# Sharing PSUM banks in the rotation and the layernorm, and a tail that waits for the last addition, in a transformer layer on eight cores

## The chip, the cores and the metric

The kernel runs on 8 cores of one Trainium2 chip, in one launch. Every core works on one sequence of 2048 tokens and holds all weights' slices in turn; the cores exchange nothing. The metric is the device time in microseconds of the slowest core. In this text PE is TensorE, DVE is VectorE, ACT is ScalarE, POOL is GpSimd, and SP is the engine from whose queue the loads of x and the stores of the output are issued.

## The reference

One layer: attention with rotary embedding on a layernormed x, then a mixture of experts (8 routed, top 2, and one shared) on a layernormed sum.

```python
def _rope(x):                      # even, odd: the two halves of the head's 128
    return concatenate([even * cos - odd * sin, even * sin + odd * cos])

q = _rope(einsum('btm,mhd->bthd', x, w_aq))
k = _rope(einsum('btm,mhd->bthd', x, w_ak))
v = einsum('btm,mhd->bthd', x, w_av)
s = einsum('bihd,bjhd->bhij', q, k) / 128 - 1e30 * causal_mask
r = einsum('bhij,bjhd->bihd', softmax(s), v) @ w_ao
...
shared_out = (silu(xf @ sw1) * (xf @ sw3)) @ sw2
cw = top-2 softmax weights of xf @ router_w.T
moe_out = einsum('te,teh,ehd->td', cw, silu(g) * u, w2)
...
x = x + attn(layernorm(x))         # 2048 x 1024 per core, 8 heads of 128
x = x + ffn(layernorm(x))          # 8 experts, 1 shared, hidden 2048
```

## The kernel before

All instructions of an engine stand in one list, in the order in which the Python code emits them, and every engine works through its list in that order. `bank_prod` emits a PE instruction that fills a PSUM bank: it waits for the tokens given to it and for everything in `bank.frees`, the instructions that read the bank since it was last filled. `bank_cons` emits a reader: it waits for the bank's last fill and adds itself to `frees`. There are eight banks, `ps[0]` to `ps[7]`, of 128 x 512 f32.

The activations are kept transposed (channels on partitions) in `x_sb` (f32) and `xn_sb` (bf16), in eight chunks of 128 channels (`kc`) by 2048 tokens, and the tokens are taken in four groups of 512 (`ts`).

The stages in order:

- x is loaded and transposed by PE through `ps[0]` and `ps[1]` (line 311), DVE copies it to `x_sb`.
- `layernorm` (lines 337 to 422), for each `ts`: DVE casts eight chunks (L355), PE sums them over the channels in `bank_s` (L364), DVE squares them (L376), PE sums the squares in `bank_q` (L380), DVE and ACT work out mean and inverse deviation on one row, PE spreads the two rows over the partitions in `bank_a` and `bank_b` (L402, L405), DVE copies these out (L408, L410), POOL scales and shifts (L415, L418). The banks alternate with the parity of `ts`. It is called twice, ahead of the attention and ahead of the experts.
- `emit_qkv_rope(h)` for each of the 8 heads, once for q and once for k, so 16 blocks. In a block PE projects all four token groups into `ps[0]` to `ps[3]` (32 matmuls, L486). Then, for each `ts`: DVE copies the bank to bf16 (L497), PE multiplies that copy by the rotation matrix into a bank of its own, `ps[4]` or `ps[5]` (L501), DVE multiplies the projection by the cosines (L506) and the rotated copy by the sines (L510), and POOL adds the two products (L514). The two products have one buffer each, so L506 of the next group waits for the POOL addition of this one (`t_rot_prev`).
- The order of the attention on PE: values of four heads, block q and block k of head 0, and then for each head `emit_passA(h)` (a bound for the softmax), `emit_qkv_rope(h + 1)`, `emit_passB(h)` (scores into `ps[4]` and `ps[5]` (L601), causal mask added by DVE (L607), exponentials by ACT (L613), product with the values (L587) and row sums (L592)). The weights of head h + 2 are requested on POOL's queue between the last two.
- Output projection, second layernorm, router.
- The experts, nine times: 16 chunks of gate and up projections (L877, L890), then eight chunks of the down projection (L938), each followed by four additions of DVE into `x_sb` (L947).
- The tail: PE transposes `x_sb` back through `ps[0]` and `ps[1]`, 128 transposes (L974), DVE copies each to a staging buffer (L980), four stores of 2 MB leave on SP's queue. The order is four groups of 512 tokens, and in each `kc` outside and the four token tiles inside; a transpose waits for the last addition of its own chunk, `t_xfinal_dc[kc]`.

Of the kernel before, what the change touches and what calls it, by code (L numbers as in the profile page):

```python
# [19 lines left out]
KC = DM // 128  # L20
# [97 lines left out]
def build_nc(dbg=False):  # L118
# [32 lines left out]
    x_sb = nc.alloc_sbuf_tensor("x_sb", [128, KC * T], F32)  # L151
# [35 lines left out]
    bigf = big[:, :].bitcast(F32)  # L187
# [3 lines left out]
    ps = [PsBank(nc.alloc_psum_tensor(f"ps{i}", [128, 512], F32).ap()) for i in range(8)]  # L191
# [32 lines left out]
    def bank_prod(bank, fn, waits=(), last=True):  # L224
        w = list(waits) + bank.frees
        toks = b.emit("tensor", fn, waits=w, incs=[(pe, 1)] if last else ())
        bank.frees = []
        if last:
            bank.ready = toks[0]
            return toks[0]  # L230
        return None
# [105 lines left out]
    def layernorm(t_x_tok, per_ts=None):  # L337
        if not isinstance(t_x_tok, list):
            t_x_tok = [t_x_tok]
        xn_tok = []  # L340
        U0 = sf[0:1, 2048:2560]
        U1 = sf[0:1, 2560:3072]
        U2 = sf[0:1, 1536:2048]
        a_rep = sf[:, 0:512]
        b_rep = sf[:, 512:1024]
        tmp = sf[:, 1024:1536]
        t_gp_prev = None
        for ts in range(NTS):
            tcol = ts * 512
            t_cp = None  # L350
            for kc in range(KC):
                col = kc * T + tcol
                t_cp = b.emit("vector",
                              lambda e, o=xn_sb[:, col:col + 512],
                              i=x_sb[:, col:col + 512]: e.tensor_copy(o, i),  # L355
                              waits=(per_ts[ts] if per_ts else t_x_tok),
                              incs=[(dv, 1)])[0]
            bank_s = ps[(ts % 2) * 2]
            for kc in range(KC):
                col = kc * T + tcol  # L360
                bank_prod(bank_s,
                          lambda e, r=xn_sb[:, col:col + 512],
                          s0=(kc == 0), s1=(kc == KC - 1):
                          e.matmul(bank_s.ap[0:1, :], onesb[:, :], r, start=s0, stop=s1),  # L364
                          waits=[t_cp], last=(kc == KC - 1))
            t_sum = bank_s.ready
            xsq = [sf[:, 2560 + i * 256: 2560 + (i + 1) * 256].bitcast(BF16)
                   for i in range(2)]
            bank_q = ps[(ts % 2) * 2 + 1]
            t_xsq_pe = [None, None]  # L370
            for kc in range(KC):
                xa = xsq[kc % 2]
                col = kc * T + tcol
                w = [t_cp, t_xsq_pe[kc % 2]]
                t_sq = b.emit("vector",
                              lambda e, o=xa, i=xn_sb[:, col:col + 512]: e.tensor_mul(o, i, i),  # L376
                              waits=w, incs=[(dv, 1)])[0]
                tokp = bank_prod(bank_q,
                                 lambda e, r=xa, s0=(kc == 0), s1=(kc == KC - 1):
                                 e.matmul(bank_q.ap[0:1, :], onesb[:, :], r, start=s0, stop=s1),  # L380
                                 waits=[t_sq], last=True)
                t_xsq_pe[kc % 2] = tokp
            t_ssq = bank_q.ready
            t1 = b.emit("vector", lambda e: e.tensor_scalar_mul(U0, bank_s.ap[0:1, :], 1.0 / DM),
                        waits=[t_sum], incs=[(dv, 1)])[0]
            bank_s.frees.append(t1)
            t2 = b.emit("vector", lambda e: e.tensor_scalar_mul(U1, bank_q.ap[0:1, :], 1.0 / DM),
                        waits=[t_ssq], incs=[(dv, 1)])[0]
            bank_q.frees.append(t2)
            b.emit("vector", lambda e: e.tensor_mul(U2, U0, U0), incs=[(dv, 1)])  # L390
            b.emit("vector", lambda e: e.tensor_sub(U1, U1, U2), incs=[(dv, 1)])
            t3 = b.emit("vector", lambda e: e.tensor_scalar_add(U1, U1, EPS),
                        incs=[(dv, 1)])[0]
            t4 = b.emit("scalar", lambda e: e.activation(U2, U1, AF.Ln),
                        waits=[t3], incs=[(ac, 1)])[0]
            t5 = b.emit("scalar", lambda e: e.activation(U1, U2, AF.Exp, scale=-0.5),
                        waits=[t4], incs=[(ac, 1)])[0]
            t6 = b.emit("vector", lambda e: e.tensor_scalar_mul(U2, U0, -1.0),
                        waits=[t5], incs=[(dv, 1)])[0]
            t7 = b.emit("vector", lambda e: e.tensor_mul(U0, U2, U1), incs=[(dv, 1)])[0]  # L400
            bank_a, bank_b = ps[4 + (ts % 2)], ps[6 + (ts % 2)]
            bank_prod(bank_a, lambda e: e.matmul(bank_a.ap[:, :], ones1[:, :], U1,  # L402
                                                 start=True, stop=True),
                      waits=[t5, t6, t_ones1])
            bank_prod(bank_b, lambda e: e.matmul(bank_b.ap[:, :], ones1[:, :], U0,  # L405
                                                 start=True, stop=True),
                      waits=[t7])
            ta = bank_cons(bank_a, "vector", lambda e: e.tensor_copy(a_rep, bank_a.ap[:, :]),  # L408
                           waits=[t_gp_prev])
            tb = bank_cons(bank_b, "vector", lambda e: e.tensor_copy(b_rep, bank_b.ap[:, :]))  # L410
            t_last = None
            for kc in range(KC):
                col = kc * T + tcol
                tm = b.emit("gpsimd",
                            lambda e, i=x_sb[:, col:col + 512]: e.tensor_mul(tmp, i, a_rep),  # L415
                            waits=[ta, t_sum, t_ssq, t_last], incs=[(gp, 1)])[0]
                t_last = b.emit("gpsimd",
                                lambda e, o=xn_sb[:, col:col + 512]: e.tensor_add(o, tmp, b_rep),  # L418
                                waits=[tb, tm], incs=[(gp, 1)])[0]
            t_gp_prev = t_last  # L420
            xn_tok.append(t_last)
        return xn_tok
# [20 lines left out]
    rope_t1 = [sf[:, 1024 + i * 512: 1024 + (i + 1) * 512] for i in range(2)]  # L443
    scale_rep = sf[:, 2048:2560]
    invl_row = sf[0:1, 2560:3072]
    invl_row_bf = sbf[0:1, 5120:5632]
    mh_row = mh_sb[0:1, 0:8]
    qb_free_tok = [None] * 2
    t_rot_prev = [None]
# [21 lines left out]
    def emit_qkv_rope(h):  # L471
        par = h % 2
        for which in range(2):
# [15 lines left out]
            for ts in range(NTS):  # L489
                sl = ts % 2  # L490
                bank = ps[ts]
                pqb = ps[4 + sl]
                qb = rope_qb[sl]
                tcs = csn[:, ts * 512:(ts + 1) * 512]
                tsn = csn[:, T + ts * 512: T + ts * 512 + 512]
                te = bank_cons(bank, "vector",
                               lambda e, o=qb, i=bank.ap[:, :]: e.tensor_copy(o, i),  # L497
                               waits=[qb_free_tok[sl]])
                qb_free_tok[sl] = bank_prod(pqb,
                                            lambda e, o=pqb.ap[:, :], r=qb:  # L500
                                            e.matmul(o, pmat_sb[:, :], r,  # L501
                                                     start=True, stop=True),
                                            waits=[te, t_pmat])
                t_t1a = bank_cons(bank, "vector",
                          lambda e, o=rope_t1[0], i=bank.ap[:, :], c=tcs:
                          e.tensor_mul(o, i, c),  # L506
                          waits=[t_cs, t_rot_prev[0]])
                t_t1b = bank_cons(pqb, "vector",
                          lambda e, o=rope_t1[1], i=pqb.ap[:, :], c=tsn:
                          e.tensor_mul(o, i, c),  # L510
# [316 lines left out]
        w2_tok[(widx, dc)] = dma(wd_w2[par], "gpsimd", dst, src, waits=[w2_free[par]])  # L827

    eo_mul_tok = [None, None]
    t_xfinal_dc = [None] * KC  # L830
    pf_w1(0, 0)
    pf_w3(0, 0)
    pf_w1(0, 1)
# [5 lines left out]
    for ei, e_ in enumerate(e_order):  # L839
# [85 lines left out]
        for dc in range(KC):  # L925
            par = dc % 2
            bset = ps[4 * (dc % 2): 4 * (dc % 2) + 4]
            for hc in range(16):
                for tsx in range(NTS):
# [8 lines left out]
                              e.matmul(o, l, r, start=s0, stop=s1),  # L938
                              waits=[w2_tok[(widx, dc)], t_eo],
                              last=(hc == 15))  # L940
            tadd = None
            for tsx in range(NTS):
                bank = bset[tsx]
                xcol = dc * T + tsx * 512
                tadd = bank_cons(bank, "vector",
                                 lambda e, o=x_sb[:, xcol:xcol + 512], i=bank.ap[:, :]:
                                 e.tensor_add(o, o, i))  # L947
            if ei == len(e_order) - 1:
                t_xfinal_dc[dc] = tadd
            w2_free[par] = (pe, pe.n)  # L950
            nxt = dc + 2
            if nxt < KC:
# [3 lines left out]
    t_final = (dv, dv.n)  # L956

    out_tiles = d["out"].rearrange("(g p) m -> p g m", p=128)
    stage = [bigf[:, 8192:12288], bigf[:, 12288:16384]]
    stage_free = [None, None]  # L960
    slot = 0
    for g4 in range(4):
        par = g4 % 2
        evac_toks = []
        for kc in range(KC):
            for ti in range(4):
                tt = g4 * 4 + ti
                bank = ps[slot % 2]
                sl = (slot // 2) % 4
                pap = bank.ap[:, sl * 128:(sl + 1) * 128]  # L970
# [1 line left out]
                bank_prod(bank,  # L972
                          lambda e, o=pap, i=x_sb[:, col:col + 128]:
                          e.transpose(o, i, identf[:, :]),  # L974
                          waits=[t_xfinal_dc[kc], stage_free[par]])
                evac_toks.append(
                    bank_cons(bank, "vector",
                              lambda e,
# [58 lines left out]
```

How the kernel before makes its waits and increments, by code:

```python
        def run(e, ws=ws, fn=fn, rincs=rincs):  # L75
            for sem, v in ws:
                e.wait_ge(sem, v)
            inst = fn(e)
            for sem, amt in rincs:
                inst = inst.then_inc(sem, amt)
```

## Time and profile before

| | |
|---|---|
| median of 12 runs | 4812.16 us (4803.93 to 5417.91) |
| the profiled execution's own time | 4818.27 us |
| its span, core 1, the slowest | 4816.7 us |
| the other cores' spans | 4797.3 to 4815.8 us |
| PE busy | 4036.8 us (84%), 16618 matmuls |
| DVE busy | 1557.1 us (32%) |
| ACT, POOL busy | 581.5 us (12%), 668.8 us (14%) |
| chain that ended last | PE 79%, DVE 12%, issue 3%, POOL 3%, ACT 2%, DMA 1% |
| mean granted TensorE clock, core 1 | 0.883 of full |

The span is the time from the first to the last instruction of a core. A busy share is taken over the whole span; the chain of work that ended last is followed back from the last instruction, at each step to what released it, and says which engine's time is on the path.

### The profile page before, as it was taken

Reading aid. Unit: us, or ns where it says so; the run is one execution under the profiler, and the core shown is the slowest. Engines: PE = TensorE matmul, PEld = TensorE weight load, DVE = VectorE, ACT = ScalarE, POOL = GpSimd, SP = SyncE. Lnnn points to the kernel's source line nnn. Section 1 sums busy time; section 2 is a strip of 40 time slices with the busy share of each in tenths; the row PEclk is TensorE's granted clock in tenths of the full one; section 3 lists DMA queues with packets and bytes.
Section 4 is the critical chain, followed back from the end, with each engine's and each line's share of the span. In section 5 each row is a group of like instructions: output and inputs, shape, how many; then the busy total and the mean of one; then the engine's idle time right before and its main releaser. Section 6 shows DMA issues by size and latency. Waiting matters only on the chain.

```text
span 4816.7 us, 48360 instructions; the slowest of 8 cores (4797.3 to 4816.7 us)
## 1 busy us (share of the span) xinstructions
PE 4036.8 (84%) x16618; PEld 1666.1 (35%) x16618; DVE 1557.1 (32%) x2517; ACT 581.5 (12%) x933; POOL 668.8 (14%) x649
## 2 busy tenths in 40 slices
PE   5266566566574699999999999999999999999998
PEld 2021112111121244444444444444444444444443
DVE  4633333333336332232332332322322322322323
ACT  0002220112220110010110110110110100100100
POOL 0621101111104310010110110110110110111100
PEclk9576677677686799999999999999999999999986
DMA  4000000000010343343343443433433434343422
GB/s 99 0 9 5 5 5 5 5 0 5 3 13 3 31 38 38 36 40 35 36 40 36 37 38 37 39 36 35 40 35 36 40 36 38 37 39 37 40 27 75
DMA packets 480622, 142.95 MB, mean 30 GB/s; under 512 B 473722, under 2 KB 476026, under 8 KB 480386
## 3 DMA queue, kind: packets, MB, share of 16 engines
q0 software_dynamic: 475488, 122.72, 27.7%
q1 hardware_dynamic: 4898, 17.14, 1.0%
q8 instruction: 141, 2.31, 0.2%
q14 instruction: 95, 0.78, 0.1%
HBM read 254.12 MB, written 8.39 MB: 54 GB/s over the span
## 4 chain that ended last, share of the span: by engine, by line
PE 79%; DVE 12%; issue 3%; POOL 3%; ACT 2%; DMA 1%; DVEq 0%; POOLq 0%; ACTq 0%; SPq 0%
PE ps L938 21%; PE ps L877 21%; PE ps L890 21%; PE ps L486 3%; DVE s_sb L622 2%; PE ps L587 2%; PE ps L592 2%; PE ps L601 2%; PE ps L626 1%; DVE xn_sb L355 1%; POOL pT L534 1%; PE ps L462 1%; ACT pT L613 1%; PE ps L671 1%; POOL big L514 1%
## 5 line engine op out<-in xcount | busy, mean ns | idle before, releaser
L877 PE MATMUL ps<-xn_sb,w_sb 128*128 128x512 bf16 x4608 | 1062.7, 384 | 5.9 <-DVE s_sb L861 3.5
L938 PE MATMUL ps<-big,w_sb 128*128 128x512 bf16 x4608 | 1029.6, 388 | 25.5 <-DVE big L912 25.5
L890 PE MATMUL ps<-xn_sb,w_sb 128*128 128x512 bf16 x4608 | 1041.5, 379 | 0.0
L907 DVE TENSOR_TENSOR s_sb<-ps,s_sb 128x512 bf16<-128x512 f32 x512 | 354.1, 692 | 1181.5 <-PE ps L890 1154.9
L221 POOL DMA_DIRECT2D w_sb<-w x360 | 333.9, 931 | 2769.6 <-PE ps L890 1778.3
L938 PEld LDWEIGHTS ps<-big,w_sb 128*128 128x128 bf16 x4608 | 458.8, 100 | 596.2 <-issue 108.0
L898 ACT ACTIVATE s_sb<-ps 128x512 bf16<-128x512 f32 x576 | 344.0, 597 | 2618.1 <-PE ps L877 2586.6
L877 PEld LDWEIGHTS ps<-xn_sb,w_sb 128*128 128x128 bf16 x4608 | 454.8, 99 | 567.7 <-issue 37.3
L890 PEld LDWEIGHTS ps<-xn_sb,w_sb 128*128 128x128 bf16 x4608 | 450.8, 98 | 543.7
L947 DVE TENSOR_TENSOR x_sb<-x_sb,ps 128x512 f32<-128x512 f32 x288 | 197.9, 687 | 857.5 <-PE ps L938 833.8
L613 ACT ACTIVATE pT<-ps,negmh 128x512 bf16<-128x512 f32 x320 | 220.0, 688 | 681.1 <-DVE ps L607 412.7
L912 DVE TENSOR_TENSOR big<-s_sb 128x512 bf16<-128x512 bf16 x576 | 245.0, 425 | 63.0 <-DVE s_sb L907 3.7
L587 PE MATMUL ps<-pT,big 128*128 128x512 bf16 x320 | 145.7, 455 | 75.8 <-ACT pT L613 64.3
L607 DVE TENSOR_TENSOR ps<-ps,maskm 128x512 f32<-128x512 f32 x128 | 89.6, 700 | 276.9 <-PE ps L601 273.9
L601 PE MATMUL ps<-big 128*128 128x512 bf16 x320 | 154.6, 484 | 20.9 <-DVE s_sb L629 11.7
L626 PE MATMUL ps<-s_sb,ones 1*128 1x512 f32 x64 | 65.3, 1121 | 117.7 <-DVE s_sb L622 117.7
L534 POOL TENSOR_TENSOR pT<-big 128x512 bf16<-128x512 bf16 x64 | 66.4, 1038 | 595.6 <-PE ps L626 545.7
L486 PE MATMUL ps<-xn_sb,w_sb 128*128 128x512 bf16 x512 | 142.3, 446 | 1.6 <-DVE big L466 1.6
L592 PE MATMUL ps<-pT,onesb 128*1 128x512 bf16 x320 | 141.0, 441 | 0.0
L501 PE MATMUL ps<-s_sb,pmat_sb 128*128 128x512 bf16 x64 | 31.8, 497 | 121.6 <-DVE s_sb L497 121.6
L622 DVE RECIPROCAL s_sb<-ps 1x512 f32<-1x512 f32 x32 | 107.1, 3346 | 62.0 <-PE ps L592 62.0
L514 POOL TENSOR_TENSOR big<-s_sb 128x512 bf16<-128x512 f32 x64 | 80.7, 1261 | 293.1 <-DVE s_sb L510 293.1
(109 smaller groups left out, 1460.4 us busy)
## 6 DMA issues: line engine op xcount, KB each, us to landing
w_sb<-w POOLq DMA_DIRECT2D x288, 256.0 KB, 6.0
w_sb<-w POOLq DMA_DIRECT2D x72, 512.0 KB, 8.0
big<-x SPq DMA_DIRECT2D x4, 2048.0 KB, 13.9
out<-big SPq DMA_DIRECT2D x4, 2048.0 KB, 7.2
w_sb<-wv POOLq DMA_DIRECT2D x2, 1024.0 KB, 19.9
w_sb<-wq POOLq DMA_DIRECT2D x8, 256.0 KB, 6.0
w_sb<-wk POOLq DMA_DIRECT2D x8, 256.0 KB, 6.6
w_sb<-wo POOLq DMA_DIRECT2D x8, 256.0 KB, 4.8
```

What stands on the lines that cost most here:

```text
L221: return b.emit(eng, lambda e, o=out_ap, i=in_ap: e.dma_start(out=o, in_=i), waits=waits, incs=[(ch, 16)], nochain=True)[0]
L486: e.matmul(o, l, r, start=s0, stop=s1),
L587: e.matmul(o, l, r, start=s0, stop=s1_),
L592: e.matmul(o, onesb[:, :], r, start=s0, stop=s1_),
L601: e.matmul(o, l, r, start=True, stop=True),
L613: e.activation(o, i, AF.Exp, bias=negmh[:, 0:1], scale=1.0 / DH),
L877: e.matmul(o, l, r, start=s0, stop=s1),
L890: e.matmul(o, l, r, start=s0, stop=s1),
L898: lambda e, o=sb_b, i=gb_.ap[:, :]: e.activation(o, i, AF.Silu),
L907: e.tensor_mul(o, i, c),
L912: e.tensor_mul(o, a, bb),
L938: e.matmul(o, l, r, start=s0, stop=s1),
```

## The change

Four edits:

1. `layernorm` uses `ps[0]` to `ps[3]` for its four banks in every token group, where it alternated between two sets.
2. In `emit_qkv_rope` the rotated copy goes back into the bank that holds the projection. For that L506 (cosines) is emitted ahead of the rotation matmul L501, and L501 waits for it.
3. The tail's transposes wait for `t_final`, the last of all additions, where each waited for the last addition of its chunk; the two loops inside a group of 512 tokens change places.
4. The tail's staging buffers are the ones of the load at the start (`bigf[:, 0:8192]`) where they were `bigf[:, 8192:16384]`. An alias that nothing uses, `invl_row_bf`, is gone.

```diff
-            bank_s = ps[(ts % 2) * 2]
+            bank_s = ps[0]
...
-            bank_q = ps[(ts % 2) * 2 + 1]
+            bank_q = ps[1]
...
-            bank_a, bank_b = ps[4 + (ts % 2)], ps[6 + (ts % 2)]
+            bank_a, bank_b = ps[2], ps[3]
...
-    invl_row_bf = sbf[0:1, 5120:5632]
...
             for ts in range(NTS):
                 sl = ts % 2
                 bank = ps[ts]
-                pqb = ps[4 + sl]
+                pqb = bank
                 qb = rope_qb[sl]
...
                 te = bank_cons(bank, "vector",
                                lambda e, o=qb, i=bank.ap[:, :]: e.tensor_copy(o, i),
                                waits=[qb_free_tok[sl]])
+                t_t1a = bank_cons(bank, "vector",
+                          lambda e, o=rope_t1[0], i=bank.ap[:, :], c=tcs:
+                          e.tensor_mul(o, i, c),
+                          waits=[t_cs, t_rot_prev[0]])
                 qb_free_tok[sl] = bank_prod(pqb,
                                             lambda e, o=pqb.ap[:, :], r=qb:
                                             e.matmul(o, pmat_sb[:, :], r,
                                                      start=True, stop=True),
-                                            waits=[te, t_pmat])
-                t_t1a = bank_cons(bank, "vector",
-                          lambda e, o=rope_t1[0], i=bank.ap[:, :], c=tcs:
-                          e.tensor_mul(o, i, c),
-                          waits=[t_cs, t_rot_prev[0]])
+                                            waits=[te, t_t1a, t_pmat])
                 t_t1b = bank_cons(pqb, "vector",
                           lambda e, o=rope_t1[1], i=pqb.ap[:, :], c=tsn:
                           e.tensor_mul(o, i, c),
...
-    t_xfinal_dc = [None] * KC
...
-            if ei == len(e_order) - 1:
-                t_xfinal_dc[dc] = tadd
...
-    stage = [bigf[:, 8192:12288], bigf[:, 12288:16384]]
-    stage_free = [None, None]
     slot = 0
     for g4 in range(4):
         par = g4 % 2
         evac_toks = []
-        for kc in range(KC):
-            for ti in range(4):
-                tt = g4 * 4 + ti
+        for ti in range(4):
+            tt = g4 * 4 + ti
+            for kc in range(KC):
                 bank = ps[slot % 2]
...
-                          waits=[t_xfinal_dc[kc], stage_free[par]])
+                          waits=[t_final, stage_free[par]])
```

## Rows read from the trace of the kernel before

**Rows 1.** Spans of the cores, and the mean granted clock

```profile
core 1: 4816.7 us, clock 0.883
```

**Rows 2.** The chain that ended last, head 1: start, duration, what

```profile
477.11 1.27 POOL big L514
...
483.26 0.70 DVE s_sb L497
...
503.96 0.71 DVE ps L607
```

**Rows 3.** Timeline, head 1, block q: start, duration, engine, line, idle before and releaser

```profile
474.62 0.69 DVE L497 CAST s_sb<-ps 128x512 bf16<-128x512 f32 x1 [7.79 <-PE ps L486]
475.42 0.69 DVE L506 TENSOR_TENSOR s_sb<-ps,csn 128x512 f32<-128x512 f32 x1
...
475.46 0.38 PE L501 MATMUL ps<-s_sb,pmat_sb 128*128 128x512 bf16 x1 [0.37 <-DVE s_sb L497]
476.21 0.69 DVE L510 TENSOR_TENSOR s_sb<-ps,csn 128x512 f32<-128x512 f32 x1
...
484.09 0.58 PE L501 MATMUL ps<-s_sb,pmat_sb 128*128 128x512 bf16 x1 [2.54 <-DVE s_sb L497]
...
484.79 0.69 DVE L506 TENSOR_TENSOR s_sb<-ps,csn 128x512 f32<-128x512 f32 x1 [0.84 <-POOL big L514]
484.90 0.15 PEld L486 LDWEIGHTS ps<-xn_sb,w_sb 128*128 128x128 bf16 x1 [0.28 <-issue]
```

**Rows 4.** Timeline, head 1, from block k's end to the scores

```profile
503.16 0.69 DVE L510 TENSOR_TENSOR s_sb<-ps,csn 128x512 f32<-128x512 f32 x1
503.96 1.50 DVE L607 TENSOR_TENSOR ps<-ps,maskm 128x512 f32<-128x512 f32 x2
...
504.00 0.59 PE L601 MATMUL ps<-big 128*128 128x512 bf16 x1 [1.32 <-DVE s_sb L510]
```

**Rows 5.** Groups by line, whole span: busy, mean ns, idle before, releasers

```profile
L601 PE MATMUL ps<-big 128*128 128x512 bf16 x320 | 154.6, 484 | 20.9 <-DVE s_sb L629 11.7 <-DVE s_sb L510 9.2
...
L506 DVE TENSOR_TENSOR s_sb<-ps,csn 128x512 f32<-128x512 f32 x64 | 44.3, 692 | 42.8 <-POOL big L514 41.1
...
L501 PE MATMUL ps<-s_sb,pmat_sb 128*128 128x512 bf16 x64 | 31.8, 497 | 121.6 <-DVE s_sb L497 121.6
```

**Rows 6.** Timeline: a matmul at full clock and the DVE instruction it releases

```profile
436.55 0.39 PE L601 MATMUL ps<-big 128*128 128x512 bf16 x1
...
437.12 0.70 DVE L607 TENSOR_TENSOR ps<-ps,maskm 128x512 f32<-128x512 f32 x1 [0.44 <-PE ps L601]
```

**Rows 7.** The same pair at half clock

```profile
508.15 0.61 PE L601 MATMUL ps<-big 128*128 128x512 bf16 x1
...
508.93 0.70 DVE L607 TENSOR_TENSOR ps<-ps,maskm 128x512 f32<-128x512 f32 x1 [0.78 <-PE ps L601]
```

**Rows 8.** The rotation matmul's line: durations in ns, minimum, median, maximum

```profile
L501 PE MATMUL ps<-s_sb,pmat_sb x64: 376/584/586, 277.8 to 1220.3; 128*128 128x512 bf16 x64
```

**Rows 9.** Stretches of L486: length, PE busy, PEld busy, granted clock

```profile
269.40:277.00 7.60, 6.78 (x31) 2.96 (x31) 1.00 0.72 86
286.80:296.10 9.30, 9.27 (x31) 3.68 (x31) 0.71 0.00 0
...
484.47:492.20 7.73, 7.73 (x31) 3.29 (x31) 0.85 0.01 2
```

**Rows 10.** Groups by line: the layernorms' channel sums

```profile
L364 PE MATMUL ps<-xn_sb,onesb 128*1 128x512 bf16 x64 | 28.2, 620 | 77.3 <-DVE xn_sb L355 77.3
```

**Rows 11.** Timeline of the start of the tail

```profile
4737.95 3.06 DVE L947 TENSOR_TENSOR x_sb<-x_sb,ps 128x512 f32<-128x512 f32 x4 [13.74 <-PE ps L938]
...
4741.12 0.69 DVE L980 COPY big<-ps 128x128 f32<-128x128 f32 x2
...
4741.56 0.72 PE L974 MATMUL ps<-identf,x_sb 128*128 128x128 f32 x2 [2.73 <-DVE big L980]
...
4742.06 0.69 DVE L980 COPY big<-ps 128x128 f32<-128x128 f32 x2 [0.25 <-PE ps L974]
```

More of the change, by code:

```diff
@@ L940, in build_nc @@
                               last=(hc == 15))
-            tadd = None
             for tsx in range(NTS):
@@ L944, in build_nc @@
                 xcol = dc * T + tsx * 512
-                tadd = bank_cons(bank, "vector",
-                                 lambda e, o=x_sb[:, xcol:xcol + 512], i=bank.ap[:, :]:
-                                 e.tensor_add(o, o, i))
-            if ei == len(e_order) - 1:
-                t_xfinal_dc[dc] = tadd
+                bank_cons(bank, "vector",
+                          lambda e, o=x_sb[:, xcol:xcol + 512], i=bank.ap[:, :]:
+                          e.tensor_add(o, o, i))
             w2_free[par] = (pe, pe.n)
```

## The prediction

> **What bounds the kernel now.** I read five views. First the spans of the cores: core 1 sets the time [rows 1]; the profiled execution took 4818.27 us, 1.6 us more than that span, and the median of twelve is 4812.16, so a sum made on the trace is a difference to carry over, not an absolute time. Second the page's busy shares: PE at 84% is the bound of the experts, which the change doesn't touch. Three of the four edits lie elsewhere, so the average says little, and I went to the stages.
>
> Third, the chain that ended last, in the stretch of head 1. In the rotation it isn't on PE: it goes L506, L510, POOL's L514, L506 and so on, then from the last bf16 copy L497 to the last rotation matmul L501 and back to PE's projections, and in block k from the last L510 to the mask addition L607 of the scores [rows 2]. The reader is to see that every member of the rotation's loop stands in the chain except L501 for the first groups: that matmul is hidden.
>
> Fourth, the timeline of one block. DVE starts L497, 0.80 us later L506, 0.79 us later L510, and PE's L501 runs beside L506 [rows 3]. L506 of group 3 starts 9.37 us after L506 of group 0 (484.79 against 475.42), so a turn takes 3.12 us: L506 to L510 0.79, L510 to POOL's start 0.90, POOL's 1.27 us and 0.16 until L506 may start. The last L501 starts 9.47 us after the first L497 (484.09 against 474.62), 0.7 us before the last L506 [rows 3]. At block k's end the mask additions start as soon as the last L510 is through (503.16, 503.96) [rows 4].
>
> Fifth, the groups by line: L506 waits 41.1 us for POOL in 48 places, 0.86 us each [rows 5]. POOL itself is busy 1.27 us of a turn and idle for the other 1.85, so neither it nor DVE is full: the loop is a ring of latencies without slack, and what is added to a turn is added to its period.
>
> **The rotation (edit 2).** No instruction is added. What changes is that L501 must wait until L506 has read the bank, and L510 must wait for L501.
>
> - Start of L506 to start of L501: L501 starts 0.84 us after the start of the DVE instruction that releases it (475.46 against 474.62) [rows 3]. L506 lasts as long as L497 (0.69 us), so I take 0.83.
> - Start of L501 to start of L510: the nearest pair is a matmul of the same shape that releases a DVE instruction. At full clock (2.4 GHz) that takes 0.57 us (436.55 to 437.12) [rows 6], at half clock (1.2 GHz) 0.78 us (508.15 to 508.93) with a matmul of 0.61 [rows 7]; an isolated one lasts 0.58 [rows 8], 0.03 less, which makes about 0.76 (I take 0.77).
> - So L506 to L510 becomes 0.83 + 0.57 = 1.40 us at full clock and 1.60 at half, where it was 0.79: +0.61 or +0.81 a turn. L497 of the next group still lies beside POOL's addition: 0.69 against 1.27.
> - Which clock: of 64 rotation matmuls the median lasts 584 ns and the shortest 376, with a mean of 497 [rows 5, 8], so 27 ran at full clock and 37 at half. The timeline has the first of each block at full clock, 0.84 us after its projections; those 6 us or later are at half. With the change the four start about 1.6, 5.5, 9.4 and 13.3 us after the first L497. I take the first as full and the others as half.
>
> Page "TensorE: Matmul & The Clock Gate" of the Trainium skill, section "Single matmul latency", puts a single cold matmul of 512 columns at (219 + 512)/1.2 = 609 ns; the trace has 584 [rows 8]. By the page 48 of the 64 would be 0.025 us dearer, 1.2 us in all, and the sum 56.1 us where it is 54.9 below; the measurement decides.
>
> Block q, where PE's next work is block k's projection, held behind the last L501 in PE's list: the last L506 is late by three turns, 0.61 + 2 x 0.81 = 2.23 us. Before, the last L501 left at 9.47; now it leaves after the last L506, at 10.17 + 2.23 + 0.83 = 13.23 (10.17 is 484.79 minus 474.62). That is 3.76 us later. Bank 3's second reading, the last L510, is over and known on PE 0.77 + 0.69 + 0.14 = 1.6 us after that L501's start (0.14 is what lies between 0.83 and 0.69 above). The projection wants the bank after L501's 0.38 us, its shortest, and three projections at one weight load per 0.43 us (0.15 + 0.28 idle) [rows 3], 1.7 us; so no further wait.
>
> Block k of heads 1 to 7, where DVE's next work is the mask addition: late by four turns, 0.61 + 3 x 0.81 = 3.04 us. The first score matmuls now start without waiting for a rotation bank, but their masks stand behind the last L510 on DVE, so nothing comes of it. For head 0 POOL's last addition releases the softmax bound, late by the same 3.04. POOL's weight requests behind the last addition move too; they are for a block a head away.
>
> Sum: 8 x (3.76 + 3.04) = 54.4 us, all on the path. Bounds: with every rotation matmul at full clock 8 x (3 x 0.61 + 1.53 + 4 x 0.61) = 46.4, with all at half 8 x (3 x 0.81 + 1.53 + 4 x 0.81) = 57.6.
>
> **What the clock may do besides.** The 32 projections behind a rotation start at half clock already: 7.73 us in one block and 9.30 in another, against 6.78 for the 31 at a granted clock of 1.00 [rows 9]. So 1 to 2.5 us are lost per block now, by where the clock comes back. A wait that is 3.8 us longer shifts that, to either side; if all eight go from the middle to an end it is 6 us more or less, and passes over the scores behind block k may move as much. I add nothing, and keep 6 us either way for the range.
>
> **The layernorms (edit 1): nothing.** The waits that sharing a bank adds are for DVE's readers L384, L387, L408 and L410 of the previous group. These stand on DVE ahead of the eight casts L355, and PE's first sum waits for the casts anyway, 77.3 us over the two calls [rows 10]. What hides the edit is DVE's own order; if the casts ran ahead of the readers, the cost would be one chain of a row per group, but they don't.
>
> **The tail (edits 3 and 4).** Before, the first two transposes run under the last four additions, and the first copy L980 starts when these end, at 4741.12. A transpose that waits releases its copy 0.50 us after its start (4741.56 to 4742.06) [rows 11]. Now the first copy comes 0.5 us later: +0.5 us. The order of the loops and the other staging area change no count, no size and no wait: every store still waits for its 32 copies. If the additions had been spread over the eight chunks, waiting for the last would cost much more, but the transposes stand on PE behind the last matmul L938, so only its four additions, 3.06 us, are left to wait for. Below nothing: the tail has no wait that the new order removes.
>
> Total 54.4 + 0.5 = 54.9 us. On the profiled execution that is 4818.3 + 54.9 = 4873.2; on the median 4812.2 + 54.9 = 4867.
>
> **Rivals.**
>
> - *The clock pays more.* The longer stretches without PE work, 13 us in place of 9.5, cost full-clock time in the projections and in the scores. Section "HAM oscillation" of the same page speaks against this change: gaps in PE's work bring the clock down, and each burst behind one starts cold. For it: PE has the most idle time just here. Against it: the clock has fallen in these gaps already [rows 8, 9]. At 1.5 us more for each of 16 blocks it is +24 us, 4890.
> - *Half of it is hidden.* Only the loop's delay counts and the last L501's new wait for L506 doesn't, because bank 3 is wanted late: 8 x (2.23 + 3.04) = 42 us, 4854. Against it: PE's list is in order, and all 32 projections stand behind L501. Rotation matmuls that stay at full clock end near the same place, 4859.
> - *No change, because the wait on L501 falls into POOL's time.* It would need POOL to be busy through the turn. It is idle 1.85 us of each 3.12, and starts 0.90 us after L510's start, as soon as that is through. Time 4812.
> - *Faster.* PE's scores wait 9.2 us for L510 to leave the rotation's banks [rows 5], and this wait is gone. If the masks followed the scores and not DVE's list, and the rotation's delay were absorbed, it is 9 us less, 4803. It decides only where the second score ends after DVE is free; in rows 4 it ends at 504.59 and its mask starts about 504.75, as soon as the first mask is through, so there is nothing to win.
>
> **How the numbers follow.** Forecast as summed, 46 to 62 us slower: 0.72. The clock pays more, 62 to 85: 0.10. Half hidden or full clock, 30 to 46: 0.13. No change, within 0.2% (9.6 us, about what a measurement of this kernel can tell from none): 0.03. Faster: 0.02. The predicted time is the likeliest, 4867. The range runs from 4848 (36 us, which takes in most of the half-hidden case less the clock's 6) to 4882 (58 at half clock, 6 from the clock, and 6 for the spread of the runs around their median); it leaves out the ends of the three others, less than 0.2. Slower 0.95, same 0.03, faster 0.02.
>
> **What would show it.** In the changed profile L510's idle in front should be about 64 x 0.8 = 51 us, released by PE's L501, where it was nearly none; L501's idle released by L506 and no longer by L497; L506's wait for POOL unchanged near 41 us; L506 turns of 3.9 us; the last L501 of a block 13.2 us after its first L497. The scores' wait for L510 should be gone with no gain. L364 should still wait for L355 alone. In the tail the first L974 starts after the last L947. The prediction is wrong if the half clock reaches the projections' whole length, if L501 to L510 takes other than 0.57 to 0.78 us, or if the order on DVE isn't what I read.

## The result, and the profile after

Slower, as forecast. The changed kernel took 4860.8 us (median of 8 runs, 4858.23 to 5376.41) where the kernel before, run beside it and earlier, has a median of 4808.2 (32 runs). In some executions, of either kernel, one die or both run at a lower clock and take some per cent longer; ratios compare the undisturbed executions alone. The ratio is 1.0112, 95% interval 1.0101 to 1.0123, which on 4808 us is 53.9 us with an interval of 48.6 to 59.1. The sum was 54.9.

The spans of the cores (span, mean granted clock), the slowest core first in the profile after:

```profile
core 4: 4858.0 us, clock 0.882
...
die 0 (median of its cores): 4855.0 us, clock 0.882
die 1 (median of its cores): 4853.3 us, clock 0.882
```

The two profiled spans differ by 41.3 us only. The profiled execution of before took 4818.3 us, 13 more than the 4805 around which most of the others lie, and its core 1 has that excess in the experts: the down projections (L938) are busy 1029.6 us there, 1012.2 on core 5 of the same execution, and 1012.4 in the profile after (L936). The medians of die 1 are 4798.2 before and 4853.3 after, 55.1 us apart. The stage of the rotation shows the difference on the two profiled cores too. From the first cosine product of the kernel to the last it was 943.2 us (277.8 to 1221.0); in the profile after L500 starts first at 278.3 and last at 1275.1, 996.8 us: 53.6 us more, so practically the whole cost lies in this stretch of the attention.

One block q of head 1 after the change, timeline (start, duration, engine, line, idle before and releaser). L496 is the copy, L500 the cosines, L504 the rotation matmul, L509 the sines, L485 the projections:

```profile
488.80 0.69 DVE L496 CAST s_sb<-ps 128x512 bf16<-128x512 f32 x1 [7.80 <-PE ps L485]
489.60 0.69 DVE L500 TENSOR_TENSOR s_sb<-ps,csn 128x512 f32<-128x512 f32 x1
490.43 0.38 PE L504 MATMUL ps<-s_sb,pmat_sb 128*128 128x512 bf16 x1 [1.16 <-DVE s_sb L500]
490.99 0.69 DVE L509 TENSOR_TENSOR s_sb<-ps,csn 128x512 f32<-128x512 f32 x1 [0.70 <-PE ps L504]
...
493.31 0.69 DVE L500 TENSOR_TENSOR s_sb<-ps,csn 128x512 f32<-128x512 f32 x1 [0.84 <-POOL big L513]
494.15 0.58 PE L504 MATMUL ps<-s_sb,pmat_sb 128*128 128x512 bf16 x1 [3.34 <-DVE s_sb L500]
494.91 0.69 DVE L509 TENSOR_TENSOR s_sb<-ps,csn 128x512 f32<-128x512 f32 x1 [0.90 <-PE ps L504]
...
502.00 0.58 PE L504 MATMUL ps<-s_sb,pmat_sb 128*128 128x512 bf16 x1 [3.34 <-DVE s_sb L500]
502.38 9.73 PE L485 MATMUL ps<-xn_sb,w_sb 128*128 128x512 bf16 x32
```

These answer to [rows 3]. The rotation matmul, which ran beside the cosine product, now stands between the two products: L500 to L509 takes 1.39 us in the first turn (489.60 to 490.99), at full clock, and 1.60 in the second (493.31 to 494.91), at half, where it took 0.79. The last rotation matmul starts 13.20 us after the first copy (502.00 minus 488.80), forecast 13.23, before 9.47. The 32 projections behind it are busy 9.73 us in this head, where 31 of them took 7.73 before [rows 9]; over the whole kernel that evens out, as the account below shows.

Block k of head 1: its first copy, its end, and the first scores (L600) and masks (L606), which answer to [rows 4]:

```profile
511.64 0.69 DVE L496 CAST s_sb<-ps 128x512 bf16<-128x512 f32 x1 [8.18 <-PE ps L485]
...
524.00 0.69 DVE L500 TENSOR_TENSOR s_sb<-ps,csn 128x512 f32<-128x512 f32 x1 [0.84 <-POOL big L513]
...
525.22 1.06 PE L600 MATMUL ps<-big 128*128 128x512 bf16 x2
525.60 0.69 DVE L509 TENSOR_TENSOR s_sb<-ps,csn 128x512 f32<-128x512 f32 x1 [0.91 <-PE ps L504]
526.40 1.50 DVE L606 TENSOR_TENSOR ps<-ps,maskm 128x512 f32<-128x512 f32 x2
```

The first copy of the same block before the change:

```profile
492.19 0.69 DVE L497 CAST s_sb<-ps 128x512 bf16<-128x512 f32 x1 [5.92 <-PE ps L486]
```

The two scores leave one after the other and wait for no product, and the masks still start where the last sine product ends: 14.76 us after the first copy (526.40 minus 511.64), before 11.77 (503.96 in [rows 4] minus 492.19).

The groups by line (busy, mean ns, idle before, releasers), which answer to [rows 5]:

```profile
L600 PE MATMUL ps<-big 128*128 128x512 bf16 x320 | 153.6, 485 | 11.7 <-DVE s_sb L628 11.7
...
L496 DVE CAST s_sb<-ps 128x512 bf16<-128x512 f32 x64 | 44.3, 692 | 128.4 <-PE ps L485 123.4
...
L500 DVE TENSOR_TENSOR s_sb<-ps,csn 128x512 f32<-128x512 f32 x64 | 44.2, 691 | 42.8 <-POOL big L513 41.1
L509 DVE TENSOR_TENSOR s_sb<-ps,csn 128x512 f32<-128x512 f32 x64 | 44.2, 691 | 54.4 <-PE ps L504 54.4
...
L504 PE MATMUL ps<-s_sb,pmat_sb 128*128 128x512 bf16 x64 | 33.4, 522 | 179.7 <-DVE s_sb L500 179.7
...
L485 PE MATMUL ps<-xn_sb,w_sb 128*128 128x512 bf16 x512 | 142.7, 447 | 1.7 <-DVE big L465 1.6
```

And three groups of the kernel before, the projections, the sine product and the copy:

```profile
L486 PE MATMUL ps<-xn_sb,w_sb 128*128 128x512 bf16 x512 | 142.3, 446 | 1.6 <-DVE big L466 1.6
...
L510 DVE TENSOR_TENSOR s_sb<-ps,csn 128x512 f32<-128x512 f32 x64 | 44.3, 692 | 7.0 <-DVE s_sb L506 0.5
...
L497 DVE CAST s_sb<-ps 128x512 bf16<-128x512 f32 x64 | 44.3, 691 | 121.7 <-PE ps L486 116.8
```

VectorE's account closes. Its idle time ahead of the sine product went from 7.0 to 54.4 us, 47.4 more, and its wait for the projections from 116.8 to 123.4, 6.6 more: 54.0 us together. The wait for POOL is 41.1 us in both, so the ring got longer and nothing else in it moved. Of the 6.6 us about 5.8 are what the forecast counted for block q: its last rotation matmul, and with it block k's projections, leaves 3.73 us late; VectorE's own chain, four longer turns, is only 3.0 us late; so VectorE waits 0.7 us more for block k's projections, eight times.

Outside the rotation matmuls the granted clock has almost no part in this. The projections are busy 142.3 us before and 142.7 after. From a block's first projection to the end of its last, single blocks move both ways, up to 1.5 us longer (this block k of head 1, 8.19 to 9.73) and up to 1.3 us shorter, and the movements cancel.

### The profile page after: what moved, and what is told of

Its sections match the earlier page's. It is cut to its first block, busy times and chain, and to the rows that moved or that the text cites. A ratio compares the mean times of both kernels' runs of the same rounds, so it can differ in the third digit from the quotient of the medians.

```text
span 4858.0 us, 48415 instructions; the slowest of 8 cores (4851.2 to 4858.0 us)
## 1 busy us (share of the span) xinstructions
PE 4019.9 (83%) x16618; PEld 1662.3 (34%) x16618; DVE 1557.0 (32%) x2517; ACT 581.4 (12%) x933; POOL 669.7 (14%) x649
## 4 chain that ended last, share of the span: by engine, by line
PE 78%; DVE 11%; issue 4%; POOL 3%; ACT 2%; DMA 1%; DVEq 1%; ACTq 0%; POOLq 0%; SPq 0%
PE ps L875 21%; PE ps L936 21%; PE ps L888 20%; PE ps L485 3%; DVE s_sb L621 2%; PE ps L586 2%; PE ps L591 2%; PE ps L600 2%; ACT pT L612 1%; PE ps L625 1%; DVE xn_sb L355 1%; POOL big L513 1%; POOL pT L533 1%; PE ps L461 1%; PE ps L670 1%
## 5 line engine op out<-in xcount | busy, mean ns | idle before, releaser
L936 PE MATMUL ps<-big,w_sb 128*128 128x512 bf16 x4608 | 1012.4, 383 | 25.5 <-DVE big L910 25.5
L936 PEld LDWEIGHTS ps<-big,w_sb 128*128 128x128 bf16 x4608 | 454.8, 99 | 583.0 <-issue 51.7
L944 DVE TENSOR_TENSOR x_sb<-x_sb,ps 128x512 f32<-128x512 f32 x288 | 197.9, 687 | 840.4 <-PE ps L936 816.8
L586 PE MATMUL ps<-pT,big 128*128 128x512 bf16 x320 | 145.3, 454 | 83.5 <-ACT pT L612 69.8
L504 PE MATMUL ps<-s_sb,pmat_sb 128*128 128x512 bf16 x64 | 33.4, 522 | 179.7 <-DVE s_sb L500 179.7
L606 DVE TENSOR_TENSOR ps<-ps,maskm 128x512 f32<-128x512 f32 x128 | 89.5, 700 | 277.1 <-PE ps L600 273.7
L600 PE MATMUL ps<-big 128*128 128x512 bf16 x320 | 153.6, 485 | 11.7 <-DVE s_sb L628 11.7
L625 PE MATMUL ps<-s_sb,ones 1*128 1x512 f32 x64 | 65.3, 1121 | 117.7 <-DVE s_sb L621 117.7
L485 PE MATMUL ps<-xn_sb,w_sb 128*128 128x512 bf16 x512 | 142.7, 447 | 1.7 <-DVE big L465 1.6
```

What stands on the lines that cost most here:

```text
L586: e.matmul(o, l, r, start=s0, stop=s1_),
L600: e.matmul(o, l, r, start=True, stop=True),
```

## The experiments

Ten kernels ran, each beside the kernel before.

**Which edit costs.** Edit 2 alone on the kernel before, and the whole change with edit 2 undone:

```diff
-                pqb = ps[4 + sl]
+                pqb = bank
...
+                t_t1a = bank_cons(bank, "vector",
...
+                          waits=[t_cs, t_rot_prev[0]])
                 qb_free_tok[sl] = bank_prod(pqb,
...
-                                            waits=[te, t_pmat])
-                t_t1a = bank_cons(bank, "vector",
...
-                          waits=[t_cs, t_rot_prev[0]])
+                                            waits=[te, t_t1a, t_pmat])
```

> The kernel before with edit 2 alone: the rotated copy goes back into the projection's bank, the cosine product stands ahead of the rotation matmul and the matmul waits for it. Theory (the wait of the matmul for the cosine product is the whole cost): 54 us slower than before, ratio 1.0113, within the error of the full change. Rival (layernorm banks or the tail carry a part): under 45 us.

> The full change with edit 2 undone: shared layernorm banks, tail that waits for the last addition, other loop order and staging area. Theory: 0.5 us slower than before, which the timing can't tell from none; the first transpose of the tail starts after the last addition and the first copy comes 0.5 us later; the channel sums still wait for the casts alone. Rival (these edits carry a part): 5 us or more slower.

Edit 2 alone: ratio 1.0113 (1.0099 to 1.0128). Without edit 2: 1.0000 (0.9988 to 1.0012). So edit 2 is the whole cost within 6 us, and the rival that the layernorm's banks or the tail carry a part is out at that size. The trace of the kernel without edit 2 shows why, at a finer grain than the timing. Groups by line, the channel sums:

```profile
L364 PE MATMUL ps<-xn_sb,onesb 128*1 128x512 bf16 x64 | 28.3, 622 | 77.3 <-DVE xn_sb L355 77.3
```

They still wait for the casts alone, 77.3 us, as in [rows 10]. And the start of its tail, timeline (L944 the additions, L967 the transposes, L973 the copies):

```profile
4724.47 3.06 DVE L944 TENSOR_TENSOR x_sb<-x_sb,ps 128x512 f32<-128x512 f32 x4 [10.75 <-PE ps L936]
...
4727.68 0.41 PE L967 MATMUL ps<-identf,x_sb 128*128 128x128 f32 x2 [2.74 <-DVE x_sb L944]
...
4728.15 0.69 DVE L973 COPY big<-ps 128x128 f32<-128x128 f32 x2 [0.62 <-PE ps L967]
```

The first copy starts 0.62 us after the last addition (4728.15 against 4727.53); in [rows 11] it was 0.11 (4741.12 against 4741.01). That is the 0.5 us of the forecast.

**The wait or the shared bank.** Order and wait of edit 2, but the rotated copy in its own bank; against the kernel with edit 2 alone:

```diff
-                pqb = bank
+                pqb = ps[4 + sl]
```

> The kernel before with the order and the wait of edit 2, but the rotated copy keeps its own bank (4 or 5). It tells the wait from the sharing. Theory (the wait alone costs): 54 us slower, as the rotation edit with the shared bank; the first scores of a head wait for the sine product again, about 9 us over the kernel, and it costs nothing because the masks stand behind that product on VectorE. Rival (reading and writing one bank in turn is itself slow, or the freed score wait is worth something): more than 3 us away from the kernel with the shared bank.

Ratio 1.0115 (1.0100 to 1.0129); its times, 4859.0 to 4860.2, lie among those of edit 2 alone, 4857.5 to 4860.6. Two groups of it:

```profile
L601 PE MATMUL ps<-big 128*128 128x512 bf16 x320 | 155.1, 485 | 15.9 <-DVE s_sb L629 11.7 <-DVE s_sb L510 4.1
...
L510 DVE TENSOR_TENSOR s_sb<-ps,csn 128x512 f32<-128x512 f32 x64 | 44.3, 692 | 54.6 <-PE ps L505 54.6
```

The sine product waits 54.6 us, as with the shared bank. The scores wait for it again, but 4.1 us and not the 9 that was expected: the last rotation matmul now leaves only 0.77 us ahead of its sine product, where it was 1.49, and the second score behind it waits 0.59 us, where it was 1.32. It costs nothing that the times show. The bank itself costs nothing either, within the 3 us over which these times spread; the order and the wait that it forces are the price.

**Is the rotation a ring on the path, and is POOL needed for the cost?** Two buffers for each of the two products, on the kernel before and on the changed one:

```diff
-    rope_t1 = [sf[:, 1024 + i * 512: 1024 + (i + 1) * 512] for i in range(2)]
+    rope_t1 = [[sf[:, 1024:1536], sf[:, 1536:2048]], [sf[:, 512:1024], sf[:, 2560:3072]]]
+    t_rot_sl = [None, None]
...
-                          waits=[t_cs, t_rot_prev[0]])
+                          waits=[t_cs, t_rot_sl[sl]])
```

One of the new buffers lies where the reciprocal of the row sums goes, so in these kernels and in the rewritten ones below the reciprocal also waits for POOL's last addition.

> The kernel before with two buffers for each of the two products of the rotation, so that VectorE doesn't wait for GpSimd's addition of the group before. Theory (the rotation is a ring of VectorE, VectorE, GpSimd that lies on the path): a turn falls from 3.12 to 3 x 0.79 = 2.38 us; block q ends 1.5 us earlier, block k 2.2, together 8 x 3.7 = 30 us faster, ratio 0.994. Rival (the rotation is only partly on the path, so that the change's cost is half hidden too): under 15 us faster.

> The full change with two buffers for each product of the rotation. The ring through GpSimd is gone, and the turn is what VectorE and the rotation matmul take one after the other: 0.79 + 1.40 or 1.60 + 0.79 = 3.0 to 3.2 us where it is 3.9. Theory (the matmul's latency adds to a turn whatever closes the ring): 19 us slower than the kernel before, so 49 us slower than the kernel before with the same two buffers. Rival (the cost needs GpSimd in the ring): less than 30 us between the two kernels with two buffers.

On the kernel before the ratio is 0.9930 (0.9912 to 0.9949), 34 us faster, 30 expected. On the changed kernel it is 1.0056 (1.0037 to 1.0074), 27 us slower than before, 19 expected. That ratio takes in the profiled execution of 4848.4 us; three other times are 4826.1 to 4826.8, 21 us above before. Between the two kernels with two buffers lie 60 us by the ratios, each of them known to 9 us either way, and 55 by the means of three low times (4826.4 and 4771.4) and by the spans of core 0 in the two profiles (4823.2 and 4768.3); 49 were expected. One turn of each, timeline; first the kernel before with two buffers (L498 the copy, L507 the cosines, L502 the rotation matmul, L511 the sines):

```profile
471.22 0.69 DVE L498 CAST s_sb<-ps 128x512 bf16<-128x512 f32 x1
...
472.02 0.69 DVE L507 TENSOR_TENSOR s_sb<-ps,csn 128x512 f32<-128x512 f32 x1
472.06 0.58 PE L502 MATMUL ps<-s_sb,pmat_sb 128*128 128x512 bf16 x1 [2.01 <-DVE s_sb L498]
472.82 0.69 DVE L511 TENSOR_TENSOR s_sb<-ps,csn 128x512 f32<-128x512 f32 x1
473.61 0.69 DVE L498 CAST s_sb<-ps 128x512 bf16<-128x512 f32 x1
```

Then the changed kernel with two buffers (L497, L501, L505, L510):

```profile
484.42 0.69 DVE L497 CAST s_sb<-ps 128x512 bf16<-128x512 f32 x1
...
485.22 0.69 DVE L501 TENSOR_TENSOR s_sb<-ps,csn 128x512 f32<-128x512 f32 x1
486.06 0.59 PE L505 MATMUL ps<-s_sb,pmat_sb 128*128 128x512 bf16 x1 [2.60 <-DVE s_sb L501]
486.82 0.69 DVE L510 TENSOR_TENSOR s_sb<-ps,csn 128x512 f32<-128x512 f32 x1 [0.91 <-PE ps L505]
487.61 0.69 DVE L497 CAST s_sb<-ps 128x512 bf16<-128x512 f32 x1
```

In the first VectorE is full, three instructions in 2.39 us, and the matmul hides under the cosines. In the second the same three take 3.19, with a hole of 0.91 us in front of the sines. So the cost doesn't need POOL in the ring: here the chain through VectorE alone, which now also has to wait for the matmul, is longer by as much. What makes the 55 where 49 were expected is not settled. In the two profiles VectorE's waits account for 51 (46.0 us at the sines, 6.9 to 52.9, and 4.9 at the copies, 121.6 to 126.5), and the projections are busy 3 to 6 us longer (140.0 and 142.3 on cores 0 and 7 of the first, 146.0 and 145.5 on cores 2 and 7 of the second), so part of it is the granted clock.

**What does the clock pay?** Eight more matmuls into an unused bank behind each of the first three rotation matmuls of a block; their results are used by nothing:

```diff
+                for _ in range(8 if ts < NTS - 1 else 0):
+                    bank_prod(ps[4],
+                              lambda e: e.matmul(ps[4].ap[:, :], pmat_sb[:, :],
+                                                 xn_sb[:, 0:512], start=True, stop=True))
                 t_t1b = bank_cons(pqb, "vector",
```

> The full change with 8 more matmuls of 512 columns into an unused bank behind each of the first three rotation matmuls of a block, results not used. It adds TensorE work in its idle time to hold the granted clock. Theory (the clock is a small part of the change's cost): the granted clock in the rotation is near full, the rotation matmuls of a turn take 0.57 to the sine product and not 0.77, 8 us in all, the projections of block k run at full clock, 10 to 15 us, so 20 to 25 us faster than the full change, 30 to 35 us slower than before. Rival (the clock pays much of the 54 us): near the time before or below. If the added matmuls run at half clock they take 3.4 us a turn, don't fit, and it gets slower than the full change.

Its two lowest times are 4840.4 and 4839.8 us, 35 us more than before and 19 to 20 less than the changed kernel's, which are 4858.2 to 4861.1; 20 to 25 were expected. They are too few for an interval. Groups by line:

```profile
L485 PE MATMUL ps<-xn_sb,w_sb 128*128 128x512 bf16 x512 | 132.3, 421 | 4.5 <-DVE s_sb L513 2.9 <-DVE big L465 1.6
...
L513 DVE TENSOR_TENSOR s_sb<-ps,csn 128x512 f32<-128x512 f32 x64 | 44.3, 692 | 45.0 <-PE ps L504 45.0
...
L504 PE MATMUL ps<-s_sb,pmat_sb 128*128 128x512 bf16 x64 | 24.1, 376 | 96.9 <-DVE s_sb L500 96.9
```

All 64 rotation matmuls run at full clock (mean 376 ns, where it was 522), and the sines' wait falls by 9.4 us, from 54.4 to 45.0; the projections are busy 132.3 us and not 142.7. With every rotation matmul at full clock the sines still wait 45.0 us where it was 7.0 before the change, and the kernel is still 35 us slower than before. The filling bounds what the clock takes in and behind the rotation of the changed kernel: about 19 us, half in the rotation matmuls and half in the projections. It doesn't say how much of that the change added, since the same filling on the kernel before was not tried. That comes from the projections' busy time, 142.3 and 142.7 us: the half in the projections was there before the change.

**A version that shares a bank in block q and beats both.** The rotation rewritten: q projects into banks 0 to 3, k into 4 to 7, the rotation matmuls of q stand among the projections of k, and VectorE does other work while a rotation matmul runs. Its order, `c` copy, `a` cosines, `r` rotation matmul, `s` sines (block, group), `p` projections of k (range of chunks):

```
c00 a00 c01 p0-2 r00 s00 a01 c02 p2-5 r01 s01 a02 c03 p5-7 r02 s02 a03 p7-8 r03 s03
c10 r10 a10 c11 r11 s10 a11 c12 r12 s11 a12 c13 r13 s12 a13 s13
```

Block q writes the rotated copy back into its own bank, with the wait of edit 2; block k uses banks 0 to 3 for it. The second version does the copies on ScalarE, and places them and the matmuls accordingly.

> A rewritten rotation: block q projects into banks 0 to 3 and block k into 4 to 7, the rotation matmuls of q stand among the projections of k, q uses the shared bank of the change, VectorE does the copy of the next group ahead of the sine product of this one, and the products have 3 and 2 buffers. Theory (what counts is what TensorE waits for, and a shared bank is free of cost where other work covers its wait): from the end of q's projections to k's last sine product 24 VectorE instructions at 0.79 us = 19.1 us where 29.2 are taken before, 80 us faster than before, ratio 0.983. Rival (sharing a bank costs by itself): under 40 us faster.

> The rewritten rotation with the bf16 copies on ScalarE, which has no other work there. Theory: VectorE has 8 instructions a block left, q's 6.4 us hide under k's projections, and 16 to 17 us are left where 29.2 are taken before: 100 us faster than before, ratio 0.979. Rival (ScalarE's copy needs a table load, or the sharing of ScalarE delays the exponentials): no faster than the rewritten rotation with the copies on VectorE.

With the copies on VectorE: 0.9837 (0.9818 to 0.9855), 78 us faster than before, 80 expected. With the copies on ScalarE: 0.9749 (0.9734 to 0.9765), 121 us faster, 100 expected. The first copy of head 1 and its last sine product, with the copies on VectorE (L500 the copy, L530 the sines):

```profile
454.68 0.69 DVE L500 CAST s_sb<-ps 128x512 bf16<-128x512 f32 x1 [9.16 <-PE ps L490]
...
464.09 0.38 PE L521 MATMUL ps<-s_sb,pmat_sb 128*128 128x512 bf16 x1 [1.15 <-DVE s_sb L510]
464.65 0.69 DVE L530 TENSOR_TENSOR s_sb<-ps,csn 128x512 f32<-128x512 f32 x1 [0.70 <-POOL big L535]
...
474.19 0.69 DVE L530 TENSOR_TENSOR s_sb<-ps,csn 128x512 f32<-128x512 f32 x1
```

And with the copies on ScalarE, on core 0 (span 4677.7 us), with the first mask behind it:

```profile
442.92 1.28 ACT L500 ACTIVATE s_sb<-ps 128x512 bf16<-128x512 f32 x2 [8.99 <-PE ps L490]
...
456.76 1.49 DVE L530 TENSOR_TENSOR s_sb<-ps,csn 128x512 f32<-128x512 f32 x2
...
458.35 1.50 DVE L668 TENSOR_TENSOR ps<-ps,maskm 128x512 f32<-128x512 f32 x2
```

From the first copy to the end of the last sine product: 29.2 us before (474.62 to 503.85 in [rows 3, 4]), 20.2 and 15.3 here. Eight heads of that are 72 of the 78 us and 111 of the 121. The projections also get faster: they are busy 128.8 us with the copies on VectorE, before 142.3.

The wait of the shared bank is covered in three groups of block q and not in the fourth. There (464.09) the rotation matmul (L521) waits 1.15 us for the cosine product (L510), and VectorE idles 0.70 us until the sine product. The view names POOL's addition as the releaser, but the sine product also starts 0.56 us after the matmul, the distance of [rows 6], so sharing costs there at most these 0.70 us a head. Block k doesn't share, and more product buffers came with the rewriting. The same kernel with banks of their own for q's rotated copies was not run, so how the 78 us divide is not shown; only that a shared bank in half of the blocks doesn't prevent them.

**Where the clock does pay.** The last version with 6 more unused matmuls behind each of the first three rotation matmuls of block k, and then with 12 more in each wait for the reciprocal of the row sums too:

```diff
+        def fill():
+            for _ in range(6):
+                bank_prod(ps[3], lambda e: e.matmul(ps[3].ap[:, :], pmat_sb[:, :],
+                                                    xn_sb[:, 0:512], start=True, stop=True))
...
+            for _ in range(12):
+                bank_prod(ps[4], lambda e: e.matmul(ps[4].ap[:, :], pmat_sb[:, :],
+                                                    xn_sb[:, 0:512], start=True, stop=True))
             bank5 = ps[5]
```

> The rewritten rotation with copies on ScalarE, and 6 more matmuls of 512 columns into an idle bank behind each of the first three rotation matmuls of block k, results not used. It holds TensorE's clock through the last of its long waits in the rotation. Theory (the clock pays little in and behind the rotation): the rotation matmuls were at full clock there already, only the first scores of a head gain, at most 1 us a head: 0 to 8 us faster than without the filling. Rival (the rotation's wait is what leaves the scores at half clock for the 22 us behind it): 20 us or more faster.

> The same with 12 more matmuls of 512 columns, results not used, also in each of the 32 waits for the reciprocal of the row sums. A quarter of the scores starts at half clock behind such a wait: an iteration takes 1.48 us there and 1.0 at full clock, for 5 to 8 iterations in each of 24 quarters. Theory (the clock is lost in the reciprocal's waits of the scores and not in the rotation): 40 to 70 us faster than the kernel filled in the rotation alone. Rival (the scores are bound by ScalarE and VectorE at either clock, or the added work is itself on the path): within 10 us of it, or slower.

Filled in the rotation: 0.9746 (0.9731 to 0.9760), the same as without, 0 to 8 us expected. Filled in both: 0.9656 (0.9640 to 0.9672), 165 us faster than before and 43 faster than the one filled in the rotation, 40 to 70 expected. Groups of the latter, the scores and the matmul that spreads the reciprocal:

```profile
L670 PE MATMUL ps<-big 128*128 128x512 bf16 x320 | 148.5, 468 | 11.4 <-DVE s_sb L699 11.4
...
L696 PE MATMUL ps<-s_sb,ones 1*128 1x512 f32 x64 | 65.3, 1121 | 117.7 <-DVE s_sb L691 117.7
```

The same two filled in both:

```profile
L670 PE MATMUL ps<-big 128*128 128x512 bf16 x320 | 136.1, 429 | 16.4 <-DVE s_sb L702 16.4
...
L699 PE MATMUL ps<-s_sb,ones 1*128 1x512 f32 x64 | 35.1, 628 | 24.6 <-DVE s_sb L691 24.6
```

The larger part of the gain is not in the scores, of which the expectation spoke, but in the spreading matmuls, 30.2 us less (65.3 to 35.1); the scores are busy 12.4 us less, the products with the values 6.8 (143.6 to 136.8) and the row sums 5.8 (140.1 to 134.3). These are busy times, which the path shows only in part. Against them the added matmuls end late by 0.2 us a wait: they and the idle time behind them are 99.8 and 24.6 us, where the idle time was 117.7.

So in the rewritten kernel the waits for the reciprocal, 32 of them, are where the granted clock is worth something. The wait in the rotation no longer is: all 64 rotation matmuls run at full clock without any filling (376 to 379 ns), and on core 0, in head 1, the granted clock is 1.00 from 442.90 to 456.00 us, from the first copy to the scores. The projections of q start below that (0.78 from 434.00 to 442.90 us), but they stand ahead of the rotation, where neither filling reaches. This is the fastest of all kernels that ran.

## Why the prediction was right

- *What bounds the stage.* That the rotation is a ring of latencies on the path, with L501 hidden, is shown by the pair with two buffers: taking POOL out gave 34 us and putting the matmul in took 55 to 60.
- *The rotation matmul's latency.* Forecast 1.40 and 1.60 us between the products, measured 1.39 and 1.60, from pairs of other lines that had the same shape.
- *The clock of the four matmuls.* Forecast one in four at full clock, 48 of 64 at half. The mean of 522 ns between 376 and 584 gives 19 at full and 45 at half: three more than assumed caught the full clock, 0.6 us.
- *Block q and block k.* 3.76 us forecast for a block q, 3.73 measured. In block k the masks start 14.76 us after the first copy, before 11.77: 2.99 late, forecast 3.04.
- *The scores' freed wait.* Gone from the trace, and without a gain: PE's idle time ahead of the product with the values rose from 75.8 to 83.5 us, so 7.7 of the 9.2 us show up one instruction later.
- *The layernorms and the tail.* Nothing and 0.5 us; the trace shows both, the timing only that they are under 6 us.
- *The clock's other part.* Kept at nothing with 6 us either way; the projections' busy time rose by 0.4 us in this pair of traces. That is partly luck: in single blocks it moved by up to 1.5 us, both ways, and the forecast gave no reason why these should cancel. With the two buffers they didn't.
- *Sum.* 54.9 forecast; 53.9 measured by the ratio, 52.6 between the medians. The predicted 4867 lies 6 us above the measured 4860.8: 4.0 of them because more runs moved the median of before from 4812.2 to 4808.2, and 2.3 because the medians differ by 52.6.

The rival "half of it is hidden" is out: edit 2 alone costs the full 54 us. "The clock pays more" is out by the same 54 us and by the projections' busy time. What stays open is the 6 us or more between 49 and 55 in the pair with two buffers.

The Trainium skill's page "TensorE: Matmul & The Clock Gate", section "HAM oscillation", says that gaps bring TensorE's clock down and that bursts behind them start cold. The traces agree, in the wait for the reciprocal, where filling it was worth 43 us. In the rotation the change made gaps longer in which the third and fourth rotation matmul of a block ran at half clock already, and only the second lost by it: it ran at full clock in 11 of 16 blocks before and in 3 after.

## What to carry to other kernels

A second PSUM bank for a small matmul whose input comes from the first was worth nothing here as a bank; its worth was that the matmul could run beside the other reader. Before sharing a bank, look in the timeline for what the matmul now overlaps with, and count the turns of the loop. Take for each the start-to-start times along the new chain (here 0.83 us from the cosines to the matmul and 0.57 or 0.77 from the matmul to the sines) less the old distance (0.79), and not the matmul's length. If a bank must be shared, put another group's work in the gap. The kernel that does so here, in half of its blocks, is faster than the one with the second bank, though it takes all eight banks and more buffers for it.

## What the runs showed that I had not expected

- Holding the clock with useless matmuls paid where a long single-row instruction of VectorE (the reciprocal, 3.35 us) stands between bursts of TensorE: 384 more matmuls, 99.8 us of PE time, made the kernel 43 us faster. The f32 matmul of one row behind it took 628 ns on average where it took 1121.
- ScalarE reads the bank and writes the bf16 copy in 0.597 us (L500, 64 times), VectorE in 0.692.
